# Cross attention on one core: another order of the TensorE, VectorE and ScalarE work inside a tile

## What is computed

```
x = x + tanh(g_xattn[0]) * attention0(ctx, layernorm(x), mask)
x = x + tanh(g_ffn[0])   * spiking_ffn(layernorm(x))
x = x + tanh(g_xattn[1]) * cross_attention(layernorm(x), ctx)      # the stage that changes
x = x + tanh(g_ffn[1])   * mixture_of_8_experts(layernorm(x))      # top-1
```

```
q, k, v = query @ Wq + bq, key @ Wk + bk, value @ Wv + bv
attn    = softmax(q k^T / 8)                 # per head, over 77 keys
out     = (attn v) @ Wo + bo + residual
return layernorm(out) * ln_gamma + ln_beta
```

## Time and profile before

| | |
|---|---|
| median of 3 runs | 878.24 us (876.4 to 881.36) |
| profiled execution, first to last instruction | 875.4 us |
| PE busy | 802.4 us (92%) |
| DVE busy | 546.3 us (62%) |
| ACT busy | 366.9 us (42%) |
| POOL busy | 373.1 us (43%) |
| mean granted TensorE clock | 0.950 |
| cross attention in the profile | from about 505 to 661 us |

### The profile page before, as it was taken

The page is one execution under the profiler, slowest core; times in us unless marked ns, Lnnn a source line. Parts: engine busy times, 40 slices in busy tenths (PEclk is TensorE's granted clock), DMA queues, the critical chain, the costliest instruction groups (busy, mean ns, idle before and its releaser), DMA issues.

```text
span 875.4 us, 13801 instructions
## 1 busy us (share of the span) xinstructions
PE 802.4 (92%) x4270; PEld 612.4 (70%) x4271; DVE 546.3 (62%) x1173; ACT 366.9 (42%) x1175; POOL 373.1 (43%) x396
## 2 busy tenths in 40 slices
PE   6888799999999899989999999999998799999995
PEld 4555445555555555548888878888886689999994
DVE  4958765777677756675998667777766433333331
ACT  4457133544354332344444366776660032222220
POOL 7256553344447364345475044444442312222221
PEclk9999599989899988999999999999998799999998
DMA  8580000000000000003600093000001364555520
GB/s 303 170 307 35 1 0 1 1 1 0 1 1 1 0 1 1 0 1 111 255 1 0 1 301 104 12 19 13 14 12 61 101 266 176 182 180 176 174 80 3
DMA packets 31887, 67.14 MB, mean 77 GB/s; under 512 B 3103, under 2 KB 22909, under 8 KB 30813
## 3 DMA queue, kind: packets, MB, share of 16 engines
q1 hardware_dynamic: 28699, 56.17, 18.3%
q0 software_dynamic: 2560, 10.17, 3.6%
q10 hardware_dynamic: 578, 0.19, 0.1%
HBM read 54.74 MB, written 12.68 MB: 77 GB/s over the span
## 4 chain that ended last, share of the span: by engine, by line
PE 67%; DVE 17%; issue 6%; ACT 3%; POOL 3%; DMA 2%; DVEq 0%; SPq 0%; ACTq 0%; POOLq 0%
PE PS L2105 9%; PE PS L2093 9%; PE PS L1488 7%; PE PS L734 6%; PE PS L1468 6%; PE PS L1296 5%; PE PS L1274 3%; PE PS L725 3%; PE PS L771 3%; PE PS L701 3%; PE PS L726 2%; DVE row_best L846 2%; PE PS L743 2%; POOL rrms L551 2%; ACT pc L1670 1%
## 5 line engine op out<-in xcount | busy, mean ns | idle before, releaser
L1055 ACT ACTIVATE EX<-PS 128x512 f32<-128x512 f32 x144 | 78.9, 594 | 133.4 <-PE PS L726 130.6
L846 DVE TENSOR_REDUCE row_best<-PS 128x1 f32<-128x1024 f32 x64 | 77.8, 1221 | 41.8 <-PE PS L701 41.5
L1015 POOL TENSOR_TENSOR sumP<-sumP,EX 128x1024 f32<-128x1024 f32 x32 | 75.7, 2364 | 43.1 <-ACT EX L1055 42.7
L1670 ACT ACTIVATE pc<-PS,mx 128x77 f32<-128x77 f32 x256 | 78.8, 359 | 26.8 <-DVE mx L1565 26.8
L2093 PEld LDWEIGHTS PS<-xeT,w 128*128 128x128 f32 x736 | 85.6, 192 | 3.6 <-DMA w<-in_L_ffn_W 1.3
L2093 PE MATMUL PS<-xeT,w 128*128 128x128 f32 x736 | 86.1, 275 | 2.0 <-DMA w<-in_L_ffn_W 1.1
L2105 PE MATMUL PS<-w,heT 128*128 x368 | 83.3, 379 | 1.3 <-DVE oe L2035 1.3
L2132 POOL DMA_INDIRECT out<-oe,target x23 | 23.2, 1011 | 126.1 <-DVE oe L2035 126.1
L734 PE MATMUL PS<-EX,V 128*64 128x512 f32 (+1 forms) x288 | 76.5, 640 | 0.0
L2105 PEld LDWEIGHTS PS<-w,heT 128*128 128x128 f32 x368 | 68.1, 190 | 10.0 <-issue 1.7
L1488 PE MATMUL PS<-vw,pcT 128*128 128x256 f32 (+1 forms) x320 | 73.0, 383 | 1.2 <-ACT pcT L1683 1.2
(11 more groups left out here) (283 smaller groups left out, 1716.1 us busy)
## 6 DMA issues: line engine op xcount, KB each, us to landing
w<-in_L_ffn_W SPq DMA_DIRECT2D x31, 1024.0 KB, 10.1
vw_rows<-vwn SPq DMA_DIRECT2D x2, 1232.0 KB
kwH_rows<-kwH SPq DMA_DIRECT2D x1, 2464.0 KB, 7.4
kwL_rows<-kwL SPq DMA_DIRECT2D x1, 2464.0 KB, 13.7
kwH<-kwH_rows POOLq DMA_DIRECT2D x1, 2464.0 KB, 12.3
kwL<-kwL_rows POOLq DMA_DIRECT2D x1, 2464.0 KB, 19.2
vw<-vw_rows SPq DMA_DIRECT2D x2, 1152.0 KB, 13.3
XR<-in_x SPq DMA_DIRECT2D x4, 512.0 KB, 13.4
```

The costliest lines, as they stand in the source:

```text
L846: dve.tensor_reduce(row_best[:, n % 2, t // GT, t % GT:t % GT + 1], PSf[:, 512 * at:512 * at + S], AX.X, ALU.max, negate=True).then_inc(ma ...
L1015: pool.tensor_tensor(sumP[:], before, EX[:, (KT * n + c) % EB, :, :], ALU.add).then_inc(pool_summed, 1)
L1055: act.activation(EX[0:r, k % EB, i, :], PS[0:r, ST_AT + i, :], ACT.Exp).then_inc(exp_done, 1)
L1670: last = act.activation(pc[:, p, h * C:h * C + C], PS[:, 1 + part, (h - h0) * C:(h - h0) * C + C], ACT.Exp, bias=mx1[:, p, h:h + 1], accum ...
```

## The change

On PE, the ten transposes of tile n's probabilities are no longer ahead of the scores of tile n+1 but one before each of the first ten of its 18 products; the two halves of `logits(n-2)` go before the products 12 and 14. `scores` starts as soon as `zcH` is there and waits for `zcL` only before the fifth product, the first that reads it. In `values`, the two transposes of x3 of tile n-1 come behind the chunks 4 and 5 and those of z of tile n+2 behind the chunks 6 and 7, and the wait for the copies is split by bank. `tp_done` counts three times a tile (after the chunks 3, 7 and 9).

On ACT, the copy of each bank waits for its own transposes: banks 4 and 5 ahead of the exponentials, bank 6 (two small copies) between the exponentials of part 0 and of part 1. On DVE, `zcL` of tile n+2 moves ahead of the residual and `keep_logits`. No instruction of computation is added or removed.

```diff
+    LOGITS_AT, X3_AT, Z_AT = (12, 14), (4, 5), (6, 7)
...
-        def scores(n, b, p):
-            pe.wait_ge(c_zT_low, n + 1)
+        def scores(n, b, p, probs=None, older=None):
+            pe.wait_ge(c_zT_ready, n + 1)
             if exists(n - 1):
                 pe.wait_ge(pexp_ready, 3 * n)
+            at = 0
             for i, (c0, c1) in enumerate(SCORES):
                 for z, w in ((zcH, kwH), (zcH, kwL), (zcL, kwH)):
+                    if z is zcL and i == 0:
+                        pe.wait_ge(c_zT_low, n + 1)
                     for k in range(KC):
+                        if probs is not None and at < HC:
+                            turn_chunk(probs, 1 - p, at)
+                        if older is not None and at in LOGITS_AT:
+                            logits_half(older, 1 - p, LOGITS_AT.index(at))
                         last = pe.matmul(PS[:, 1 + i, 0:c1 - c0], z[:, p, k * P:k * P + P], w[:, k, b, c0:c1],
                                   start=w is kwH and z is zcH and k == 0, stop=z is zcL and k == KC - 1)
+                        at += 1
                 last.then_inc(sc_done, 1)
...
+        def turn_chunk(n, p, c):
+            if c == 0:
+                pe.wait_ge(first_norm, n + 1)
+            if c in FULL_OF_PART:
+                pe.wait_ge(pnorm_ready, 2 * n + 1 + FULL_OF_PART.index(c))
...
+            if c % 4 == 3 or c == HC - 1:
+                ins.then_inc(tp_done, 1)
...
-            pe.wait_ge(tp_act, 4 * n + 4)
             for c, (c0, c1) in enumerate(ctx_chunks):
                 r = c1 - c0
+                if c % 4 == 0:
+                    pe.wait_ge(tp_act, 4 * n + (c // 4 + 1 if c < 8 else 4))
                 ins = pe.matmul(PS[:, 7, 0:D], pcT[0:r, c, :], vw[0:r, b, c, :], start=c == 0, stop=c == HC - 1)
+                if c in X3_AT and x3_of is not None:
+                    x3_half(x3_of, 1 - p, X3_AT.index(c))
+                if c in Z_AT and z_of is not None:
+                    z_half(z_of, p, Z_AT.index(c))
             ins.then_inc(pvc_done, 1)
...
         def body(b, n, p):
-            turn_probs(n, p)
+            older = n - 2 if exists(n - 2) else None
             if exists(n + 1):
-                scores(n + 1, b if not isinstance(n, int) else (n + 1) // TB, 1 - p)
-            if exists(n - 2):
-                logits(n - 2, p)
-            values(n, b, p)
-            if exists(n - 1):
-                turn_x3(n - 1, 1 - p)
-            if exists(n + 2):
-                turn(n + 2, p)
+                scores(n + 1, b if not isinstance(n, int) else (n + 1) // TB, 1 - p, probs=n, older=older)
+            else:
+                for c in range(HC):
+                    turn_chunk(n, p, c)
+                if older is not None:
+                    logits(older, p)
+            values(n, b, p, n - 1 if exists(n - 1) else None, n + 2 if exists(n + 2) else None)
...
 # DVE body
+            if exists(n + 2):
+                cross_z_low(dve, n + 2, p)
             residual(n, p)
             if exists(n - 2):
                 keep_logits(n - 2, p)
-            if exists(n + 2):
-                cross_z_low(dve, n + 2, p)
             residual_stats(n, p)
...
 # ACT body
-            copy_probs(n)
+            copy_bank(n, 0)
+            copy_bank(n, 1)
             if exists(n + 1):
-                for part in range(3):
-                    numerators(n + 1, 1 - p, part)
+                numerators(n + 1, 1 - p, 0)
+            copy_rest(n)
+            if exists(n + 1):
+                numerators(n + 1, 1 - p, 1)
+                numerators(n + 1, 1 - p, 2)
             if exists(n + 2):
                 copy_turned(n + 2, p)
```

More of the change, by code:

```diff
@@ L1452, in pe_cross, with z_half @@
     def pe_cross(pe, begin=False):
+        def z_half(n, p, k):
+            if k == 0:
+                pe.wait_ge(c_z, n + 1)
+                if exists(n - 1):
+                    pe.wait_ge(c_zT_low, n)
+            ins = pe.transpose(PS[:, 0, k * P:k * P + P], zc[:, p, turned_cols(k)], ident[:])
+            if k == KC - 1:
+                ins.then_inc(c_zT, 1)
         def turn(n, p):
-            pe.wait_ge(c_z, n + 1)
-            if exists(n - 1):
-                pe.wait_ge(c_zT_low, n)
@@ L1457, in turn @@
             for k in range(KC):
-                last = pe.transpose(PS[:, 0, k * P:k * P + P], zc[:, p, turned_cols(k)], ident[:])
-            last.then_inc(c_zT, 1)
-        def scores(n, b, p):
-            pe.wait_ge(c_zT_low, n + 1)
+                z_half(n, p, k)
+        def scores(n, b, p, probs=None, older=None):
+            pe.wait_ge(c_zT_ready, n + 1)
             if exists(n - 1):
                 pe.wait_ge(pexp_ready, 3 * n)
+            at = 0
             for i, (c0, c1) in enumerate(SCORES):
@@ L1480, in values @@
-        def values(n, b, p):
+        def turn_chunk(n, p, c):
[3 more added lines that the diff above has]
+                pe.wait_ge(pnorm_ready, 2 * n + 1 + FULL_OF_PART.index(c))
+            c0, c1 = ctx_chunks[c]
+            ins = pe.transpose(PS[0:c1 - c0, 4 + c // 4, c % 4 * P:c % 4 * P + P], pc[:, p, c0:c1], ident[:])
+            if c % 4 == 3 or c == HC - 1:
+                ins.then_inc(tp_done, 1)
+        def values(n, b, p, x3_of, z_of):
@@ L1489, in values, with x3_half @@
+                if c in Z_AT and z_of is not None:
+                    z_half(z_of, p, Z_AT.index(c))
             ins.then_inc(pvc_done, 1)
+        def x3_half(n, p, k):
+            if k == 0:
+                pe.wait_ge(x3_ready, n + 1)
+                if exists(n - 1):
+                    pe.wait_ge(x3T_ready, n)
+                pe.wait_ge(c_zT_low, n + 3 if exists(n + 3) and exists(n + 2) else NT)
+            ins = pe.transpose(PS[:, 0, D + k * P:D + k * P + P], x3[:, p, k * P:k * P + P], ident[:])
+            if k == KC - 1:
+                ins.then_inc(x3T_done, 1)
@@ L1491, in turn_x3, with logits_half @@
         def turn_x3(n, p):
[L1492 to L1495, removed]
             for k in range(KC):
-                last = pe.transpose(PS[:, 0, D + k * P:D + k * P + P], x3[:, p, k * P:k * P + P], ident[:])
-            last.then_inc(x3T_done, 1)
+                x3_half(n, p, k)
+        def logits_half(n, p, k):
+            if k == 0:
+                pe.wait_ge(x3T_ready, n + 1)
+                pe.wait_ge(lg_ready, n + 1)
+                if exists(n + 1):
+                    pe.wait_ge(res_ready, n + 2)
+            ins = pe.matmul(PS[:, 7, D:D + E], x3T[:, p, k * P:k * P + P], wr[:, k, :], start=k == 0, stop=k == KC - 1)
+            if k == KC - 1:
+                ins.then_inc(lg_done, 1)
@@ L1500, in logits, with body @@
         def logits(n, p):
-            pe.wait_ge(x3T_ready, n + 1)
-            pe.wait_ge(lg_ready, n + 1)
+            for k in range(KC):
+                logits_half(n, p, k)
+        def body(b, n, p):
+            older = n - 2 if exists(n - 2) else None
             if exists(n + 1):
[L1504 to L1507, removed]
@@ L1509, in body @@
-        def body(b, n, p):
-            turn_probs(n, p)
-            if exists(n + 1):
-                scores(n + 1, b if not isinstance(n, int) else (n + 1) // TB, 1 - p)
-            if exists(n - 2):
-                logits(n - 2, p)
-            values(n, b, p)
-            if exists(n - 1):
-                turn_x3(n - 1, 1 - p)
-            if exists(n + 2):
-                turn(n + 2, p)
+                scores(n + 1, b if not isinstance(n, int) else (n + 1) // TB, 1 - p, probs=n, older=older)
[4 more added lines that the diff above has]
+                    logits(older, p)
@@ L1676, in copy_x3T, with copy_bank, copy_rest @@
             act.activation(x3T[:, p, :], PS[:, 0, D:2 * D], ACT.Copy).then_inc(x3T_ready, 1)
-        def copy_probs(n):
-            act.wait_ge(tp_done, n + 1)
+        def copy_bank(n, i):
+            act.wait_ge(tp_done, 3 * n + i + 1)
+            act.activation(pcT[:, 4 * i:4 * i + 4, :].rearrange("p c n -> p (c n)"), PS[:, 4 + i, :],
+                           ACT.Copy).then_inc(tp_act, 1)
+        def copy_rest(n):
+            act.wait_ge(tp_done, 3 * n + 3)
             r = HK - 9 * P
[L1681 to L1684, removed]
+            act.activation(pcT[:, 8, :], PS[:, 6, 0:P], ACT.Copy).then_inc(tp_act, 1)
+            act.activation(pcT[0:r, 9, :], PS[0:r, 6, P:2 * P], ACT.Copy).then_inc(tp_act, 1)
         def body(b, n, p):
-            copy_probs(n)
+            copy_bank(n, 0)
+            copy_bank(n, 1)
             if exists(n + 1):
-                for part in range(3):
-                    numerators(n + 1, 1 - p, part)
+                numerators(n + 1, 1 - p, 0)
+            copy_rest(n)
+            if exists(n + 1):
+                numerators(n + 1, 1 - p, 1)
+                numerators(n + 1, 1 - p, 2)
             if exists(n + 2):
```

## The result

The changed kernel takes 873.36 us in the median of 18 runs, the kernel before 879.11 in as many on the same chip; the ratio is 0.9946 with a 95% interval of 0.9926 to 0.9966, a gain of 4.7 us (3.0 to 6.5); the two medians themselves lie 5.75 us apart. The forecast was 4.0 us (874.2).

What follows compares the result with a forecast made beforehand. PE was taken to set 9.7 us in four unrolled periods, the ACT and DVE loop 9.99 in eight looped ones. Gains 3.4 + 1.1 less 0.5 make 4.0 us, 878.24 to 874.2, range 869.8 to 880.5.

Steps and rivals of the forecast that it cites:

- The bound and the relay: On PE, z transpose, `zcH`, `x3T`, `zcL` cost 0.4 to 0.45 us of a 10.1 us unrolled period; without them 9.7.
- the 0.1 more for the first pair of products: On PE, the first pair of score products was read as taking about 0.1 us more after the gap.
- Alternation costed at nothing: On PE, placing small products between wide ones was taken as zero; bounds 0.28 us gained or 1.1 to 2.2 lost a tile.
- The longer loop: ACT and DVE, `zcH` to `zcH`: 9.54 us in unrolled bodies, 9.99 in looped ones, against PE's 9.7.
- The sum: Whole kernel: 3.4 us from twelve periods plus 1.1 at the head less 0.5 at the tail, 4.0 us gained.
- the head: Before the twelve periods: scores of tile 3 start at 521.1 instead of 522.16, 1.1 us gained.
- The tail: Last tile: values wait for x3, residual 15 about 16.4 us after the last scores, 0.5 lost; copies by bank cannot show.
- PE-bound throughout: Rival: DVE's slow issue partly hides, all twelve periods 9.7 us, 116.4 together, kernel 871.9 us; chance 0.24.
- The one in which the changes give all back: Rival: copies and longer DVE block make the loop 0.2 us longer, looped periods 10.19, kernel 875.9 us; chance 0.16.
- The slower one: Rival: weight loads show where transposes and products alternate on PE, 0.09 us each, kernel 885 or about 898 us; chance 0.14.

Runs made afterwards that it cites:

- r2: Kernel before with only the `zcL` wait moved to ahead of the fifth score product: twelve periods 116.31 us, ratio to the kernel before 0.9897.
- r6: Changed kernel with the x3 and z transposes back behind the values: twelve periods 125.80 us, ratio to the kernel before 1.0026.
- r3: Changed kernel with the ten probability transposes back ahead of the score products: twelve periods 117.52 us, ratio to the kernel before 0.9915.
- r7: Changed kernel with the hardware loops written out, all bodies unrolled: twelve periods 116.43 us, ratio to the kernel before 0.9914.
- r4: Changed kernel with bank 6's two small copies ahead of the exponentials: twelve periods 117.28 us, ratio to the kernel before 0.9915.
- r9: Kernel before with the `zcL` wait moved, copies by bank and DVE's new order: twelve periods 117.95 us, ratio to the kernel before 0.9893.
- r8: Kernel before with only the `zcL` wait moved and copies and their waits by bank: twelve periods 116.30 us, ratio to the kernel before 0.9905.

## Why the prediction was right

**The bound and the relay: right.** Four unrolled periods were forecast at 9.7 and are 9.69 to 9.72. The relay's 0.4 us leave PE's path, and r2 shows that the moved wait does it, r6 that `zcH` needs a cover. One small reading was wrong: the 0.1 more for the first pair of products is no restart behind a gap. In r2 PE never waits and its first pair takes 0.51 all the same (577.02 to 577.53), behind ten transposes that take 1.01 and not 1.10. The 0.1 belongs to the transposes, and the sum for a tile stays.

**Alternation costed at nothing: right to 0.05 us a tile.** A pair takes 0.32 where the parts take 0.21 and 0.11, and the unrolled periods are at most 0.05 longer than those of r3. The rule of the Trainium skill that I set against it (TensorE: Matmul & The Clock Gate, Part 3, Packing small matmuls: weight loads overlap running products only in another row group) does not describe these traces: a pair with two loads for all 128 rows takes the 0.32 us of its two parts, so neither seam, into the product or out of it, shows a load.

**The longer loop: right, and it is the heart of the matter.** Forecast 9.99 in looped bodies, their periods have a mean of 9.92 (10.45 at most). r7 removes the looped bodies' slow issue, r4 the copies, r9 adds DVE's order alone, and each moves the periods as that loop says. That the one loop shown from an unrolled body reads 9.54, the figure forecast, is luck: PE's transpose released its second `zcH` 0.08 us late, so the loop by itself was 9.46.

**The sum: a little low.** Twelve periods 4.0 against 3.4, the head 1.3 against 1.1 (tile 3's scores start 16.90 us after the last update of x instead of 18.19), the tail -0.4 against -0.5: 4.85 against 4.0. The term that was mis-sized is "loop 9.99, above PE's 9.7" for the looped bodies: the eight periods have a mean of 9.92, which is the 0.6 us. In the looped tile shown above the loop is 10.44 with a stretch of 2.76 in it, so its fixed part is 7.68, where I had summed 7.71: from `zcH` to the residual's statistics it takes 1.88 us (538.24 to 540.12), forecast as 0.85 + 0.34 + 0.75 = 1.94. That explains about half. The rest I did not test. The rows show one part of it: behind the longest tile the loop from `zcH` to `zcH` is 9.84 (548.68 to 558.52), but the period is 9.73, because PE follows the first `zcH` by 0.67 us and the second by 0.56.

**The tail: right in size, and in the wait for x3.** Residual 15 was forecast 16.4 after the last scores and is 16.30, with the wait for x3 in the middle of the values as foretold. Two things in it were wrong. The copies by bank do show behind this wait: started 2.84 us after the transposes, as before, the values would have come to the x3 transpose at about 652.0 and not at 651.21 (an estimate from the rows above, 647.04 + 2.84 + five chunks, 2.15). Copies by bank are worth 1.4 us (r8 against r2) and the x3 transposes among the values cost 0.75 (r6). The loss of 0.4 that is left is mostly the place of the mark, with nine more transposes, 1.0 us, behind it, and part of the head's gain is the same shift. Counted from the first transpose of tile 14 the last stretch is 17.32 us before and 16.30 after, a gain. And one step was named wrongly: the residual of tile 14 came at 9.69 instead of 9.9, held by PE's values (its bracket says 0.23 us) and not by the last division.

**The rivals.** PE-bound throughout did not happen in the change; r7, r2 and r8 show what it would have been, 116.3 to 116.4, the 116.4 of that rival. The one in which the changes give all back had looped periods of 10.19; they have a mean of 9.92. The slower one is excluded by the 0.32 a pair. What I did not see before: that the forecast's own parts name a better kernel. The gap needs one wait moved; everything else either pays for the alternation (the z transposes, DVE's order) or is useful only in the last tile (the copies). r8, which has only the moved wait and the copies, is 8.15 us faster than before in this stage, against the 4.85 of the change.

## What to carry to other kernels

When an engine waits at the head of a group of products for the last link of a relay, first ask which product reads that link and move only this wait; the block that stood ahead of the group is the cover for the earlier links, and breaking it up takes the cover away. Work pulled ahead of something else on a second engine goes onto that engine's loop: add that loop up before and after, in the slowest of the bodies, because here DVE's stretch was 0.1 to 0.9 us longer in the hardware loop's bodies than in the unrolled ones. Where medians differ by less than their scatter, measure the changed stage in the profile between two events that both kernels have.

## What had not been expected of the hardware

Two logits between two products of 308 columns take 0.50 us with them (572.45 to 572.95); logits and products in separate groups would be 0.18 + 0.28 = 0.46. Logits between wide products cost here 0.04 more a pair, not less. Transposes between the values go the other way. From the timeline of r2, where nothing is interleaved (L1470 scores, L1490 values, L1479 the next transposes of probabilities):

```profile
577.53 0.58 PE L1470 MATMUL PS<-kwL,zcH 128*128 128x462 f32 x2
...
579.64 0.44 PE L1470 MATMUL PS<-kwH,zcH 128*128 128x308 f32 x2
...
580.84 4.57 PE L1490 MATMUL PS<-vw,pcT 128*128 128x256 f32 x20
...
585.68 1.26 PE L1479 MATMUL PS<-ident,pc 128*128 128x128 f32 x10
```

Products of 308 columns and logits take 1.20 us in r2 (579.64 to 580.84) and 1.29 in the changed kernel (572.45 to 573.74); values with the four transposes of x3 and z take 4.84 in r2 (to 585.68) and 4.76 in the changed kernel (573.74 to 578.50). The two nearly cancel, and r3, which has both, has three unrolled periods of 9.66 to 9.67, as r2 has. So the 0.03 us by which the changed kernel's 9.70 is above r2's 9.67 goes with the ten alternated transposes.

The looped bodies' cost is uneven and repeats: the longest period is the same one in every profile of the changed kernel (10.44 to 10.47, between the scores of tiles 5 and 6, with the step from one loop iteration to the next in DVE's stretch of that tile), with 0.56 us in which DVE waits for nothing but its own issue. The kernel before has the same 0.56 at the same place.
